# An order of steps for each engine, expert steps split in two, spacers between scatters, and fewer filler products, in a two-layer transformer kernel

## What is computed

```python
x = x + _L0_xcond_ref(_layernorm(x), ctx, ctx, tau, delta, Wq, bq, Wk, bk, Wv, bv, Wo, bo)
x = x + _L0_ffn_ref(_layernorm(x), gate_W, gate_b, wi_W, wi_b, wo_W, wo_b, lora_A, lora_B)
x = x + _L1_xcond_ref(_layernorm(x), ctx, ctx, tau, delta, Wq, bq, Wk, bk, Wv, bv, Wo, bo)
x = x + _L1_ffn_ref(_layernorm(x), switch_w, switch_b, w1, b1, w2, b2)
# attention:        scores = (q @ k.T * tau + delta) / sqrt(8);  softmax(scores) @ v;  @ Wo.T + bo
# feed-forward 0:   top1 = argmax(x @ gate_W.T + gate_b);  relu(x @ wi_W.T + wi_b + lora[top1]) @ wo_W.T + wo_b
# feed-forward 1:   routes = argmax(x @ switch_w + switch_b);  (gelu(x @ w1[routes] + b1) @ w2[routes] + b2) * max prob
```

## Time and profile before

| | us |
|---|---|
| runs: 198.54, 197.87, 196.61, median | 197.87 |
| the profiled execution, its own time | 196.75 |
| its span, first to last instruction | 194.9 |
| TensorE products busy, by the profile | 164.1 |
| VectorE busy | 122.1 |
| ScalarE busy | 97.4 |
| GpSimd busy | 75.5 |
| mean granted clock of TensorE | 0.973 |

### The profile page before, as it was taken

One profiled execution on the slowest core, in us unless ns is written; L12 is line 12 of the kernel. 1 busy time (PEld: TensorE's weight loads), 2 busy tenths in 40 slices (PEclk: granted clock), 3 DMA queues, 4 the chain that ended last, 5 costly groups with the idle time before them and its releaser, 6 DMA issues.

```text
span 194.9 us, 3393 instructions
## 1 busy us (share of the span) xinstructions
PE 164.1 (84%) x880; PEld 112.7 (58%) x881; DVE 122.1 (63%) x360; ACT 97.4 (50%) x228; POOL 75.5 (39%) x96
## 2 busy tenths in 40 slices
PE   7894699989988978678897989995678999999930
PEld 2542555646735733454573455633367999999920
DVE  2689845859663559977433998374567666655420
ACT  5392427845562363452327554465255576766700
POOL 8899160000400066020002001016204889888871
PEclk9999669999999999999999999999999999999996
DMA  6400007000000599940000000002640273100000
GB/s 189 159 3 4 4 5 246 6 0 3 5 4 7 143 330 405 531 171 0 3 0 0 0 0 0 0 3 97 180 138 31 82 194 123 32 18 10 22 26 2
DMA packets 14483, 15.48 MB, mean 79 GB/s; under 512 B 6842, under 2 KB 11205, under 8 KB 14400
## 3 DMA queue, kind: packets, MB, share of 16 engines
q1 hardware_dynamic: 12944, 13.29, 21.2%
q0 software_dynamic: 1088, 1.60, 2.5%
q10 hardware_dynamic: 432, 0.37, 0.7%
HBM read 13.50 MB, written 5.44 MB: 97 GB/s over the span
## 4 chain that ended last, share of the span: by engine, by line
PE 56%; DVE 20%; issue 9%; ACT 4%; POOL 4%; DMA 3%; POOLq 0%; SPq 0%; ACTq 0%; DVEq 0%
PE acc L1005 10%; PE scores L1098 9%; PE acc L1109 8%; PE scores L990 4%; PE shared L1052 4%; DVE MR L756 4%; DVE QG L746 4%; PE shared L965 3%; PE acc L903 3%; PE shared L1038 3%; PE shared L945 3%; POOL out L542 2%; PE shared L917 2%; PE shared L1025 2%; DVE XN L708 2%
## 5 line engine op out<-in xcount | busy, mean ns | idle before, releaser
L1005 PE MATMUL acc<-P,VP 123*128 123x512 f32 (+1 forms) x80 | 41.6, 620 | 0.6 <-ACT P L620 0.6
L620 ACT ACTIVATE P<-scores 123x512 f32<-123x512 f32 (+1 forms) x40 | 23.0, 595 | 22.3 <-PE scores L990 21.9
L666 ACT ACTIVATE HT<-scores,B 128x128 f32<-128x128 f32 x88 | 25.3, 369 | 12.7 <-PE scores L1098 10.0
L756 DVE TENSOR_REDUCE MR<-shared 128x4 f32<-128x308 f32 x64 | 26.8, 471 | 4.9 <-PE shared L965 4.5
L522 POOL TENSOR_TENSOR X<-X,ROWS 128x512 f32<-128x512 f32 x6 | 8.1, 1345 | 52.4 <-DVE XN L708 52.2
L990 PE MATMUL scores<-QG,KG 102*123 102x512 f32 (+1 forms) x48 | 23.1, 530 | 2.6 <-ACT QG L612 1.2
L542 POOL DMA_INDIRECT out<-XS,token x22 | 22.7, 1031 | 4.2 <-issue 4.0
L1098 PE MATMUL scores<-XST,HT 128*128 128x128 f32 x176 | 23.6, 277 | 0.8 <-ACT XST L659 0.8
L965 PE MATMUL shared<-KG,QG 98*128 98x308 f32 x64 | 21.5, 399 | 3.0 <-DVE MR L756 1.1
L1109 PE MATMUL acc<-W,HT 128*128 x176 | 23.1, 276 | 0.2 <-issue 0.2
L1098 PEld LDWEIGHTS scores<-XST,HT 128*128 128x128 f32 x176 | 21.4, 192 | 1.3 <-ACT XST L659 1.2
(11 more groups left out here) (121 smaller groups left out, 238.8 us busy)
## 6 DMA issues: line engine op xcount, KB each, us to landing
...
slots<-in_empty SPq DMA_DIRECT2D x1, 2860.0 KB, 14.2
...
```

Of the source, the lines that this page charges most:

```text
L620: act.activation(P[0:w, n % NP], scores[n % 2][0:w, :], ACT.Exp).then_inc(probs_ready, 1)
L666: ins = act.activation(HG1[:, t % NHB, c], hidden[t % 2][:, c], ACT.Gelu_apprx_tanh, bias=B1[:, bass.ds(expert[t] * NF + k, 1)])
L756: dve.tensor_reduce(MR[:, b, qt, g, 2:2 + HG], bank(s)[:, 0:GK].rearrange("p (h k) -> p h k", h=HG), AX.X, ALU.max).then_inc(max_read, 1)
L1005: pe.matmul(acc[half][:, :], VP[0:w, l, b, j, half], P[0:w, n % NP, :], start=(j == 0), stop=(j == NT - 1)).then_inc(probs_used, 1)
```

## The change

Each of TensorE, ScalarE, VectorE and GpSimd gets a table of its own. The bank of a product follows TensorE's table alone. What a step does is as before, but for this:

- `moe/t` is split. On TensorE and ScalarE `m1/t` is the transpose of tile t+1, the first product and the gelu, and `m2/n` the second product. On VectorE `cw/n` is the weight copy, `bs/n` the bias sum and `m2/n` the last sum. On GpSimd `pb/n` makes bias rows, `row/b/i` is one row scatter and `so/n` one output scatter.
- The first weight has four copies instead of three, the bias rows 11 buffers instead of six.
- `gap/i` on GpSimd is a spacer: a memset of 128x384 elements that GpSimd then awaits. Three stand between the row scatters of batch 0, the others between scatters that have no `pb` between them.
- The filler products are nine at the opening, in the other accumulator, and none later.
- `prob/b` has become the first part of `rank/b` on VectorE.
- The reciprocal root of `ln/3/0` moves from GpSimd's power to ScalarE. `ln/3/1` stays on GpSimd.
- The wait for all of the second expert weights moves from `moe/-1` to `m2/0`.

```diff
+NPB = NSB
-WARM = 13
-BRIDGE_Q, BRIDGE_X = 14, 14
+WARM = 9
-NWC = 3
-NPB = 6
-AHEAD = NQ
+NWC = 4
+
+TABLES = {
+    "pe": """
...
+        pv/0/1/5 sc/0/1/7 pv/0/1/6 sc/0/1/8 ut/0 sc/0/1/9 pv/0/1/7 hid/0/0:4 pv/0/1/8:10 out/0 wo/0/1 xt/2/0 vp/1
+        q/1/0/0 xt/1/1 max/1/0/0:4 gate/1 max/1/0/4:7 ut/1 max/1/0/7 q/1/0/1 hid/1/0:3 max/1/0/8 mt/1/0/0 hid/1/3
...
+    "pool": """
...
+        row/0/2 gap/2 row/0/3 pb/0 ln/3/1 pb/1:6 so/0 pb/6:8 so/1 pb/8:11 row/1/0 gap/3 row/1/1 gap/4 row/1/2 gap/5
...
-            for s in steps:
-                if s[0] == "ln" and s[1] == 3:
+            for s in orders["pool"]:
+                if s == ("ln", 3, 1):
...
-                elif s[0] == "rank":
-
-                    b = s[1]
-                    if b == 1:
-                        bias_of(0)
-                    pool.wait_ge(preset, 16)
...
+                elif s[0] == "row":
+
+                    _, b, i = s
+                    if i == 0:
+                        pool.wait_ge(preset, 16)
+                        pool.wait_ge(slot_ready, b + 1)
+                        pool.wait_ge(p_ready, b + 1)
+                    i += b * NQ
...
+                elif s[0] == "gap":
+                    finish(pool.memset(XN[:, 0, 0:3], 0.0), spaced)
+                elif s[0] == "pb":
+                    bias_of(s[1])
+                elif s[0] == "so":
...
+                elif kind == "cw":
+                    n = s[1]
+                    if n == 0:
                         dve.wait_ge(in_moe, 48)
+                        dve.wait_ge(x_ready, nth["out", 1] + 1)
                         for e in range(E):
                             dve.wait_ge(in_w1[e], 16)
...
             pe.wait_ge(idle_ready, 1)
-            keep_busy(WARM)
-            for s in steps:
+            keep_busy(WARM, acc[1])
+            for s in orders["pe"]:
...
-                    if s == ("q", 0, 0, 1):
-                        keep_busy(BRIDGE_Q)
...
-                        keep_busy(BRIDGE_X)
```

More of the change, by code:

```diff
@@ L107, in schedule @@
 def schedule():
[L116 to L149, removed]
-    for s in steps:
[L151 to L154, removed]
+    orders = {}
@@ new lines, in schedule, with order @@
+    for engine, table in TABLES.items():
+        orders[engine] = []
+        for entry in table.split():
+            entry, _, end = entry.partition(":")
+            kind, *index = entry.split("/")
+            index = [int(i) for i in index]
+            for i in range(index[-1], int(end) if end else index[-1] + 1):
+                orders[engine].append((kind, *index[:-1], i))
+    return orders
+def order(orders):
+    nth = {}
+    for steps in orders.values():
+        counts = {}
+        for s in steps:
+            kind = "x" if s[0] in ("wo", "out") else s[0]
+            n = counts[kind] = counts.get(kind, -1) + 1
+            nth[s] = max(n, nth.get(s, 0))
+            if s[0] == "ln" and s[1:] != (3, 1):
+                n = counts["act_ln"] = counts.get("act_ln", -1) + 1
+                nth["act_ln", s[1], s[2]] = max(n, nth.get(("act_ln", s[1], s[2]), 0))
@@ L181, in build @@
 def build(nc, x, ctx, att0, att1, consts, small, rows, ffn0w, loraB, sw, w1, b1, w2, b2, empty, out):
-    steps = schedule()
-    use = banks(steps)
-    nth = order(steps)
+    orders = schedule()
+    use = banks(orders["pe"])
+    nth = order(orders)
     before = {}
@@ L563, in _ @@
             act.wait_ge(zeroed, 1)
-            for s in steps:
+            for s in orders["act"]:
                 kind = s[0]
@@ L681, in _ @@
             dve.memset(idle[:, :], 1.0).then_inc(idle_ready, 1)
-            for s in steps:
+            for s in orders["dve"]:
                 kind = s[0]
@@ L899, in _, with keep_busy @@
             expert = {}
-            def keep_busy(n):
+            def keep_busy(n, unread):
                 for _ in range(n):
-                    pe.matmul(acc[0][:, :], idle[:, 0:128], idle[:, 0:S], start=True, stop=True)
+                    pe.matmul(unread[:, :], idle[:, 0:128], idle[:, 0:S], start=True, stop=True)
             pe.wait_ge(idle_ready, 1)
-            keep_busy(WARM)
-            for s in steps:
+            keep_busy(WARM, acc[1])
+            for s in orders["pe"]:
                 kind = s[0]
@@ L930, in _ @@
                             ins.then_inc(full[use[key][0]], 1)
+                elif kind == "busy":
+                    _, late, n = s
+                    if late:
+                        pe.wait_ge(on_ready, 2 * 2 * B - 1)
+                    keep_busy(n, acc[1 - late])
                 elif kind == "vp":
@@ L1070, in _ @@
                     ins.then_inc(full[use[s][0]], 1)
-                elif kind == "moe":
+                elif kind == "m1":
                     t = s[1]
                     if t == -1:
-                        for e in range(E):
-                            pe.wait_ge(in_w2[e], 16)
                         for i in (2, 3):
```

158 lines of the change are left out of this document (93 added, 65 removed).

## The result

| | before | changed |
|---|---|---|
| median of the runs, us | 197.43 (196.61 to 198.54, 4 runs) | 202.07 (200.87 to 203.15, 4 runs) |
| profiled execution, us | 196.75 | 202.19 |
| its span, us | 194.9 | 200.4 |
| mean granted clock of TensorE | 0.973 | 0.888 |

The ratio is 1.023, with a 95% interval of 1.015 to 1.031: slower by 1.5 to 3.1%, where 193.6 us was forecast. 202.07 lies above the range. A fourth execution puts the median of the kernel before at 197.43; the forecast started from 197.87. In all tables the median is over every execution of a kernel, while the ratio leaves out those that fell in a slower state of the chip, which matters for e3 (201.01 without one of 203.61) and e8 (193.50 without one of 323.01).

The account below looks back on a forecast made before the run. It took the chain of dependent steps through batch 0, ending in GpSimd's scatters, as the bound. Terms 0 + 0.5 - 11.2 + 1.3 + 1.2 + 0 + 3.0 + 1.0 = -4.2 gave 192.5, median 193.6 us; range 187.5 to 199.

Parts of the forecast that it names:

- Opening and layer 0: Start through feed-forward 0 of batch 0: fewer fillers cost 0 (bounds -1.5 and +2), layer 0 +0.5 us.
- Attention of layer 1: Layer 1, batch 0, first maximum to stage 3 statistics: 33.8 us instead of 45.0, term -11.2.
- the 10 named as a sign of failure: VectorE idle over 10 us in the layer 1 stretch would show the forecast wrong.
- the clock's own 3.0: Slow TensorE clock in layer 1, doubling a query product and half of batch 1's feed-forward: +3.0 us, bounds 0 and +6.
- the walk: Following the new tables step by step, each step starting when engine and inputs are free; first tile at 130.0.
- Routing to the first tile: Stage 3 statistics to first expert tile: term +1.3 us, three spacers +1.1 of it; tile expected near 131 to 135.
- the terms for exposed maxima, the root and the handoffs: Before the first tile: exposed maxima +0.9 us, root on ScalarE -0.7, handoffs that a walk misses +1.2.
- First tile to the row scatter of batch 1: Start of experts: 12.1 us instead of 9.4, the power standing behind tile 0's bias rows; slow clock +1.0, bounds 0 and +3.5.
- the rival in which the gain goes to the scatters: Batch 1's first row scatter pushed from 12.1 to 16 us behind the first tile: +3.5, 197 us; chance 0.13.
- The scatters, the step that failed: GpSimd at the end: 23 intervals of 1.66 us, 38.2 in all; a spacer bounded by 0 and 0.6.
- The clock: Rival: TensorE's clock falls and stays low from 70 through batch 1's feed-forward, first expert tiles +3.5: 203 us, chance 0.15.
- The empty table: Rival: the table's load on SP comes late and the first row scatter waits: about 195 us, chance 0.06.

Follow-up runs that it names:

- e3: Changed kernel with the power of stage 3 of batch 1 put ahead of the first bias row on GpSimd, spacers kept: 201.87 us.
- e8: e2 with 13, 6 and 5 filler products added on TensorE in the waits at layer 1's start: 193.78 us.
- e12: Kernel before without its two sets of 14 bridging fillers, the 13 opening ones kept: 199.72 us.
- e11: e9 with batch 1's route earlier, its power and row scatters earlier on GpSimd, and the layer 1 fillers of e8: 190.67 us.
- e2: Changed kernel without the six spacers between row scatters, the nine between output scatters kept: 194.63 us.
- e5: e2 with ten filler products on TensorE in front of the first expert tile: 193.22 us.
- e6: e2 with batch 1's power ahead of the first bias row, and its transposes and route one expert step earlier on TensorE and VectorE: 196.86 us.
- e9: Changed kernel with ten fillers in front of the first expert tile and none of the 15 spacers: 188.14 us.
- e1: Changed kernel without any of its 15 spacers: 195.11 us.
- e14: Changed kernel with every spacer writing 8 elements instead of 384, its wait kept: 195.18 us.

## Why the prediction was wrong, step by step

The forecast put the last output scatter at 189.82 - 4.2 = 185.6; it starts at 195.36. The 9.8 us between, by the prediction's own steps:

- *Opening and layer 0.* Right for the place: the first maximum of layer 1 at 75.02, forecast 74.7. That fewer bridges cost nothing there is not confirmed: in the kernel before they hold 0.7 us up to the first maximum of layer 1 (e12), within the bounds given.
- *Attention of layer 1.* Right in sum, and it is the change's real gain: work on VectorE 25.95 (forecast 26.5), idle 10.9 (7.3 plus 3.0 for the clock), length 36.8 (33.8 plus 3.0). The idle time crosses the 10 named as a sign of failure, but that sign had left the clock's own 3.0 out; the statistics fall at 111.8, within 109 to 113. Out product of batch 1 at 89.2, low clock from 70 to 84: both as said. Part of the match is luck: e11, with the clock mostly held, takes 34.7 us where the walk had 33.8, and the clock costs the 2.0 us between 34.7 and 36.7 instead of 3.0.
- *Routing to the first tile.* 134.69, within 131 to 135, and 0.5 later than the terms ahead of it add up to. Two errors nearly cancel in it, which is luck: the three spacers cost 3.1 (7.2 us over the four starts, 4.1 in e2), not 1.1, while statistics to first row scatter took 11.15 us (11.34 before), 1.6 less than the 12.7 that the terms for exposed maxima, the root and the handoffs make of it. Which of the three was too large is not shown.
- *First tile to the row scatter of batch 1.* Forecast 12.1 plus 1.0 for the clock; measured 14.9, so 1.8 is lost. The reason given, the power behind the bias row, is wrong: e3 moved it and nothing followed. The slow clock and TensorE's order, in which the route stands behind the first tiles' products, hold it by 1.4 us (e5) and, moved together with the power, by 1.1 us (e6). Of the 1.8, 0.4 is the walk (12.5 in e9 where 12.1 was forecast), 0.4 the clock (13.9 in e1 against 12.5 in e9, so 1.4 where 1.0 was counted; in the kernel before e12 gives 2.1), and 1.0 goes with the spacers (14.9 against 13.9). That is half of the rival in which the gain goes to the scatters (12.1 to 16 us behind the first tile, a move of 3.9 that it prices at 3.5).
- *The scatters, the step that failed.* "With its wait the scatter interval becomes about 1.65" took a spacer for 0.38 us. It is 0.93, above the bound of 0.6: 1.65 leaves 0.68 beside the scatter's own 0.97 for the memset and the wait behind it, and they take 0.44 and 0.79. By its own row (0.31 us for 248 elements) the memset alone would have been 0.48. And "23 x 1.66" gave one price to intervals with a bias row and with a spacer. 45.7 instead of 38.2: 7.5 us of the 9.8, all but 0.2 of it in the 12 intervals with a spacer.
- *The clock* was a rival with 203, near the result by number. But its mechanism is not what ran: the clock came back at 84. Its "first expert tiles" part is real, and so is a third fall at 160, which nobody forecast and which is gone without the row spacers (e2) or with short ones (e14).
- *The empty table* was issued at 103.41 and needs 13.9 us, so it has landed by 117.3; the first row scatter starts at 122.93 and does not wait for it.

With the spacers out alone (e1) the time is 195.1, in the range, and with the fillers back as well (e9) 188.1: 4.4% under the kernel before. The rest of the edit is a gain; its parts (each engine's own order, the added buffers, the moved root and waits) were not told apart.

What stays open: the pause in e1 before 151, and one of the same kind in e2. ScalarE and VectorE start together at 149.75, 3.3 us behind the end of the products they need (145.35 + 1.06), and TensorE then waits for ScalarE. No row names a cause, and e5, e8 and e9 don't have it. The price of the low clock in layer 1 rests on the one profile of e11, in which the clock was not held throughout.
